# Splitting GpSimd's weight subtraction into two halves of 512 columns

## The reference

```python
x = x + gnn(layernorm(x), edges, W, b)       # h = x W^T + b; sum over 10000 edges + self, scaled by degrees
h = layernorm(x) @ lin0_w + lin0_b
h = silu(h @ swi1_w1 + b1) * (h @ swi1_w2 + b2)
# mixture of experts: 8 experts, the 4 best for each token, and a shared expert of width 2048
routed = sum_e combine[:, e] * ((silu(h @ w1[e]) * (h @ w3[e])) @ w2[e])
h = routed + (silu(h @ sh_w1) * (h @ sh_w3)) @ sh_w2
h = h @ lin1_w + lin1_b
h = silu(h @ swi2_w1 + b1) * (h @ swi2_w2 + b2)
out = x + h
```

## Time and profile before

| | |
|---|---|
| median of three runs | 1656.29 us |
| profiled execution | 1656.63 us |
| its span | 1655.0 us |
| PE busy | 1606.2 us, 97% |
| DVE busy | 491.9 us, 30% |
| ACT busy | 520.2 us, 31% |
| POOL busy | 783.8 us, 47%; of it L392 713.6 us in 296 instructions |
| DMA | 205.62 MB, mean 124 GB/s |

### The profile page before, as it was taken

The page is one execution under the profiler, slowest core; times in us unless marked ns, Lnnn a source line. Parts: engine busy times, 40 slices in busy tenths (PEclk is TensorE's granted clock), DMA queues, the critical chain, the costliest instruction groups (busy, mean ns, idle before and its releaser), DMA issues.

```text
span 1655.0 us, 28056 instructions
## 1 busy us (share of the span) xinstructions
PE 1606.2 (97%) x11047; PEld 1588.0 (96%) x11047; DVE 491.9 (30%) x898; ACT 520.2 (31%) x745; POOL 783.8 (47%) x396
## 2 busy tenths in 40 slices
PE   6889989999999999999999999999999899999997
PEld 5789889999999999999999999999999899999997
DVE  5865621111541011414132242424221044111011
ACT  4312123222222234334444434444444222222120
POOL 1211023332352465766767586767677566333330
PEclk8999999999999999999999999999999999999999
DMA  4301032223232254645555464646465566233220
GB/s 128 125 27 39 1 126 77 77 68 126 73 99 77 87 152 130 205 141 183 155 176 170 147 202 140 209 141 209 152 185 156 154 180 181 77 104 111 71 74 34
DMA packets 64355, 205.62 MB, mean 124 GB/s; under 512 B 13228, under 2 KB 14478, under 8 KB 64248
## 3 DMA queue, kind: packets, MB, share of 16 engines
q1 hardware_dynamic: 44718, 157.88, 32.1%
q0 software_dynamic: 14976, 32.81, 6.4%
q10 hardware_dynamic: 4554, 13.32, 2.2%
HBM read 185.01 MB, written 18.95 MB: 123 GB/s over the span
## 4 chain that ended last, share of the span: by engine, by line
PE 91%; DVE 3%; issue 2%; DMA 1%; POOL 1%; ACT 1%; SPq 0%; POOLq 0%; DVEq 0%; ACTq 0%
PE acc L1323 84%; PE acc L1298 2%; DMA rows<-x_dram 1%; PE acc L1603 1%; PE acc L1582 1%; POOL gath L436 1%; POOL w_lo L392 1%; PE acc L1370 0%; DVE yrow L769 0%; DVE gath L801 0%; PE acc L1438 0%; DVE gath L795 0%; DVE gath L793 0%; PE acc L1651 0%; PE acc L1468 0%
## 5 line engine op out<-in xcount | busy, mean ns | idle before, releaser
L392 POOL TENSOR_TENSOR w_lo<-raw,w_hi 128x1024 fp32r<-128x1024 f32 x296 | 713.6, 2419 | 761.6 <-ACT w_hi L384 756.0
L1323 PE MATMUL acc<-act_b,w_hi 128*128 128x314 f32 (+8 forms) x2560 | 518.6, 311 | 0.0
L1323 PE MATMUL acc<-act_x,w_hi 128*128 128x344 f32 (+7 forms) x2048 | 451.7, 309 | 2.3 <-POOL w_lo L392 1.7
L1323 PEld LDWEIGHTS acc<-act_b,w_hi 128*128 128x128 f32 x2560 | 409.9, 189 | 0.0
L1323 PE MATMUL acc<-act_a,w_hi 128*128 128x314 f32 x1792 | 353.3, 314 | 11.3 <-issue 5.4
L1323 PEld LDWEIGHTS acc<-act_x,w_hi 128*128 128x128 f32 x2048 | 342.3, 188 | 3.9 <-issue 3.2
L1323 PE MATMUL acc<-act_b,w_lo 128*128 128x314 f32 (+8 forms) x1280 | 332.1, 308 | 0.0
L384 ACT ACTIVATE w_hi<-raw 128x1024 fp32r<-128x1024 f32 x296 | 310.7, 1050 | 46.2 <-PE acc L1323 34.8
L1323 PE MATMUL acc<-act_x,w_lo 128*128 128x344 f32 (+7 forms) x1024 | 316.3, 309 | 0.0
L1323 PEld LDWEIGHTS acc<-act_a,w_hi 128*128 128x128 f32 x1792 | 288.6, 193 | 12.2 <-issue 5.6
L1323 PEld LDWEIGHTS acc<-act_b,w_lo 128*128 128x128 f32 x1280 | 225.1, 189 | 0.0
(11 more groups left out here) (189 smaller groups left out, 884.1 us busy)
## 6 DMA issues: line engine op xcount, KB each, us to landing
raw<-stream_dram SPq DMA_DIRECT2D x296, 512.0 KB, 3.7
y_dram<-yrow POOLq DMA_DIRECT2D x16, 512.0 KB
rows<-x_dram ACTq DMA_DIRECT2D x2, 2500.0 KB
y_dram<-yrow POOLq DMA_DIRECT2D x8, 352.0 KB
rows<-x_dram SPq DMA_DIRECT2D x5, 500.0 KB
x_dram<-rows ACTq DMA_DIRECT2D x1, 2500.0 KB
h_rows_dram<-rows ACTq DMA_DIRECT2D x1, 2500.0 KB
out_dram<-rows ACTq DMA_DIRECT2D x1, 1250.0 KB
```

What stands on the lines that cost most here:

```text
L392: nc.gpsimd.tensor_tensor(w_lo[:, s, :], raw[:, s, :], w_hi[:, s, :].bitcast(f32), ALU.subtract).then_inc(lo_split, 1)
L1323: ins = pe.matmul(o, w, xs_[h], start=(first and w is hi and xs_ is x_hi), stop=(last and w is lo))
```

## The change

`split_lo` subtracts 512 columns, then the other 512, in two instructions. The second has no wait of its own; the count `lo_split` goes up when it is done, so PE and SP see one event for each unit as before.

```diff
@@ -389,8 +389,11 @@
                 nc.gpsimd.wait_ge(hi_split, u + off + 1)
             else:
                 nc.gpsimd.wait_ge(hi_split, u + (off + 1))
-            nc.gpsimd.tensor_tensor(w_lo[:, s, :], raw[:, s, :], w_hi[:, s, :].bitcast(f32),
-                                    ALU.subtract).then_inc(lo_split, 1)
+            for c0 in (0, D // 2):
+                c = slice(c0, c0 + D // 2)
+                last = nc.gpsimd.tensor_tensor(w_lo[:, s, c], raw[:, s, c], w_hi[:, s, c].bitcast(f32),
+                                               ALU.subtract)
+            last.then_inc(lo_split, 1)
```

## The result

The changed kernel takes 1650.55 us (median of 11 runs, 1649.63 to 1654.29) against 1656.60 us for the kernel before on the same chips; the ratio is 0.997 with a 95% interval of 0.9961 to 0.9979. So it is faster, by 3.5 to 6.5 us; the medians differ by 6.05. The prediction was 1649.3 us in a range of 1647.0 to 1657.5.

A forecast was written before the change was run, and what follows sets the result against it. PE is busy 97% of the span and rarely waits for the split, but POOL's long instruction stops DVE, for which PE waits. 5.3+2.4-0.4 = 7.3 us under 1656.63 gives 1649.3 us, range 1647.0 to 1657.5.

The forecast's parts named there:

- The mechanism: In the graph layer, DVE operations with inputs in SBUF wait for POOL's current instruction to end; halves admit them sooner.
- Rival 1: POOL keeps the ports over both halves, so DVE is blocked as before: 1657.0 us, chance 0.21.
- What a half costs: Fixed part 0.07 us per instruction, bounds 0.04 to 0.30; a half takes 1.21 us, a pair 2.42, each admission 0.08 more.
- Part A, the decoding: First decoding, 54 to 76 us: a round costs two halves, 2.58 us; L791 2.6 us earlier, first one-hot 3.7.
- The stall behind it: POOL's unit at 66.77 us holds a later one-hot and PE waits: 1.0 us taken back, 2.1 at the bad end.
- Part A, the clock's place in the sum: No clock fall at 68.75 to 75.60 us: 2.6 us won, added to 2.7 for 5.3 in all, bounds 0.2 and 6.
- Part B: Single DVE blocks at 93, 126 and 147 us: PE waits of 0.74, 0.7 and 0.95 go, 2.4 us; bad end 1.0.
- L770 follows it without a gap: At 93 us L770 directly behind L769 keeps POOL out, so PE's whole 0.74 us wait goes.
- The reading of L801 at 113.70: L769 behind it needs the ports too and waits for the second half until about 116.4 us: nothing won.
- the one at 147: L801 at 147.13 us is followed by L825, which reads PSUM: all 0.95 us of PE's wait goes.
- Part C: Six expert starts, where PE waits for the first unit: dearer pairs cost 0.4 us, bounds 0.2 and 1.8.
- Rival 3: Slower: at expert starts DVE's L1137 goes in between halves, each start loses 0.69 us: 1660.7 us, chance 0.06.

The follow-up runs named there:

- the partial kernels: Halves in only some units, whole instructions elsewhere: graph layer only 1650.81 us, all but the graph layer 1658.14, units 1 to 4 1651.43, units 5 to 9 1653.83.
- quarters: Four instructions of 256 columns for each of the eleven graph-layer units, whole ones elsewhere: 1646.44 us, ratio 0.9940 to the kernel before.
- the kernel with the unit ahead: Whole instructions as before, but in experts 1 to 6 POOL subtracts the first outstanding unit ahead of store and gathers: 1653.33 us, 0.9982 of the kernel before.

## Why the prediction was right, and where it was not

- **The mechanism** was right: DVE is let in at the end of a half. Rival 1, that POOL keeps the ports over a pair, is refuted in the graph layer by the rows at 54 to 63 us, and the partial kernels place the gain there. At the expert starts what spoke for rival 1 stayed true: DVE was kept out over the whole backlog. PE shows no wait for DVE there, before or after.
- **What a half costs**: 0.07 us of fixed part was too little. Eight halves with DVE let in took 10.51 us, 1.31 each, against 1.29 forecast; where DVE is kept out, behind the gathers, a pair takes 2.50 us start to start against 2.35 for a whole one, so 0.15. The bounds held.
- **Part A, the decoding**: forecast 2.6 us earlier for L791 and 3.7 for the first one-hot. Measured 2.7 (65.32 against 68.03) and 3.8 (66.57 against 70.40), less 0.3 by which the whole stretch lay earlier in this execution. The boundaries were all met, with nothing to spare in place of 0.14 us: L796 took 0.38 instead of 0.32, so it stood at the boundary for some 0.06. The stall behind it was 1.34 us (1.0 forecast), for a partly different reason: the unit at 66.77 was said not to move, but it came at 68.05, since ACT waited for its load. The clock did not fall, as forecast.
- **Part A, the clock's place in the sum**: the 2.6 us were won where forecast, but I took the clock's other falls as fixed. They are not. The kernel with halves in the graph layer only runs the same instructions there as the changed kernel, and its profile has 10.2 us at the low level in that window where the changed kernel's has 17.1: behind the same wait of PE (3.17 and 3.16 us) the low stretch lasted 3.4 us in the one and 6.8 in the other. In the profiled execution the low stretches at 113 and 150 us grew by 3.4 us each and took the gain back. The runs near 1650 us have no profile; their mean clock is 0.003 higher, which over 1650 us is an estimate of 10 us less at half rate, or up to 5 us of work, enough for the 3.9 us that part the medians of the groups. At 91 us, ahead of those falls, A's 5.3 us measured 4.5: PE's wait there ends 96.06-91.15 = 4.9 us earlier, less the 0.3, less 0.1 that is B's.
- **Part B**: forecast 2.4, measured 0.14+0.12+0.95 = 1.2. The step that failed is "L770 follows it without a gap", which was to keep POOL out as the run of L1085 did. The second half was already waiting when L772 went in, and it took the ports at its end; L773 then took 1.30 us where it takes 0.35 alone. Of the signs named, PE's waits at 95 and 128 us were to be gone and stayed at 0.60 and 0.61. I had named this as B's bad end with 1.0. The reading of L801 at 113.70 (nothing won where the next DVE operation needs the ports as well) was right, and the one at 147 (all 0.95) too: both follow from what comes next on DVE. The mistake was to treat L770 otherwise than L769 behind L801.
- **Part C**: forecast 0.4, measured 0.9 us of added waits (1.7 to 2.6). Direction right, mis-sized by the fixed part: from the first to the last matmul of an expert's first products PE took 0.11 to 0.18 us longer at each of the six starts.
- **Rival 3** asked for 0.69 us a start. It was 0.15, and DVE was never let in.

The sum of 7.3 us stands against 6.1 by the medians and 2.7 in the profiled execution. That the total was near is in part luck: B and C were 1.7 us too good together, and by the profiles the clock can give or take more than that.

## What to carry to other kernels

Where DVE and GpSimd contend, read what DVE does next: cutting GpSimd's instruction pays if the operation behind the blocked one reads PSUM or has work before it needs the ports again, and is worth little if it needs them at once (0.14 of 0.74 us with halves, 0.44 with quarters). Cut only where PE waits on DVE, and leave GpSimd's instructions whole where PE waits on GpSimd; there, put the unit that PE needs ahead of the DMA issues. A change of 3 us in a program of 1650 is of the size of one stretch of 6.8 us at the low TensorE clock, so read the granted clock of every profile before a term of the sum is believed.

## What the runs showed of the hardware

- At the ends of back-to-back GpSimd subtractions DVE is let in during the graph layer (a half there then takes 1.34 to 1.37 us instead of 1.29), and in the experts at the backlog from 1055.85 us on, but not in the backlog right behind the gathers: at none of seven boundaries in 10.59 us, and the same at all six starts (10.23 to 10.70 us). What makes the difference stays open. The time since the last gather's issue does not (5 us in the kernel with the unit ahead), nor does the gathers' data: in the changed kernel it had landed by 1047.77 us, and two more boundaries passed. The kernel without the gathers had no such backlog left to show it.
- The Trainium skill, SBUF — State Buffer, section "SBUF: two separate sides", has the lock held for the whole instruction of whoever starts first. The rows agree that an instruction is not broken into. The section does not say who is next when both engines have an instruction waiting, so the rows behind the gathers do not deny it, and the prediction read too much into it where it took rival 1 to be out by it.
- A waiting GpSimd half goes in between two DVE instructions that follow each other without a gap (L772, L773 at 88 us), yet ten L1085 in a row kept one out for 2 us. Why is open.
- A late start of a unit costs PE more than its idle row: 0.75 against 0.53 us at expert 5.
